# A graph layer on one core: layer 2 of the inner pairs with W2 standing and a split input, and half of the sums added by GpSimd

## What is computed

```python
h = jnp.maximum(_layernorm(x, axis=-1), 0.0)
agg = jax.ops.segment_sum(edge_attr, receivers, num_segments=N_NODES)   # receivers = dst
z = jnp.concatenate([agg, h], axis=1)
hid = jax.nn.relu(z @ W1 + b1)       # W1: 256 x 512
out = x + hid @ W2 + b2              # W2: 512 x 128
```

## Time and profile before

| | |
|---|---|
| median of 3 runs | 201.23 us |
| the profiled execution, its own time | 201.16 us |
| its span, first to last instruction | 199.3 us |
| PE busy, DVE busy, ACT busy, POOL busy | 96%, 66%, 43%, 22% |
| moved by DMA | 62.47 MB |
| granted TensorE clock, mean | 1.0 (2.4 GHz) |

### The profile page before, as it was taken

One profiled execution on the slowest core, in us unless ns is written; L12 is line 12 of the kernel. 1 busy time (PEld: TensorE's weight loads), 2 busy tenths in 40 slices (PEclk: granted clock), 3 DMA queues, 4 the chain that ended last, 5 costly groups with the idle time before them and its releaser, 6 DMA issues.

```text
span 199.3 us, 6821 instructions
## 1 busy us (share of the span) xinstructions
PE 190.6 (96%) x2568; PEld 163.2 (82%) x2568; DVE 131.8 (66%) x582; ACT 86.5 (43%) x188; POOL 43.4 (22%) x119
## 2 busy tenths in 40 slices
PE   7897899998999999999999999999999999999994
PEld 5586789776797898898898898898897898898894
DVE  2865775666877677678568669588487388575221
ACT  3454526433624634623714714813813704823440
POOL 6592202202211202210220220221121121220000
PEclk9999999999999999999999999999999999999999
DMA  6999999999999999999999999999999995010011
GB/s 203 382 374 378 362 373 377 375 375 377 376 377 376 375 379 383 383 392 387 381 378 388 377 385 380 376 385 378 341 376 378 311 376 167 4 53 3 0 53 44
DMA packets 44628, 62.47 MB, mean 313 GB/s; under 512 B 1822, under 2 KB 44300, under 8 KB 44594
## 3 DMA queue, kind: packets, MB, share of 16 engines
q1 hardware_dynamic: 44264, 61.66, 87.2%
q10 hardware_dynamic: 330, 0.36, 0.5%
HBM read 58.81 MB, written 3.20 MB: 311 GB/s over the span
## 4 chain that ended last, share of the span: by engine, by line
PE 79%; DMA 15%; SPq 2%; DVE 1%; issue 1%; DVEq 0%
PE bank L867 21%; PE bank L938 20%; PE bank L907 17%; PE bank L917 15%; DMA edges<-in_edge_attr 15%; PE bank L882 3%; PE bank L891 2%; SPq L303 1%; SPq L297 1%; DVE aggT L623 1%; DVE w_lo L642 0%; PE bank L860 0%; SPq L306 0%; PE bank L837 0%; SPq L327 0%
## 5 line engine op out<-in xcount | busy, mean ns | idle before, releaser
L867 PE MATMUL bank<-edges,onehot 128*32 128x128 f32 x1656 | 52.2, 275 | 2.7 <-DMA edges<-in_edge_attr 1.6
L867 PEld LDWEIGHTS bank<-edges,onehot 128*32 128x32 f32 x1656 | 43.1, 110 | 10.2 <-issue 6.2
L623 DVE TENSOR_TENSOR aggT<-bank,aggT 128x32 f32 x277 | 35.7, 190 | 22.2 <-issue 10.2
L458 ACT ACTIVATE hidden<-bank,b_col 128x512 f32<-128x512 f32 (+2 forms) x56 | 34.2, 634 | 35.9 <-PE bank L917 35.8
L938 PE MATMUL bank<-w,hidden 128*128 128x128 f32 (+1 forms) x392 | 47.6, 278 | 0.0
L938 PEld LDWEIGHTS bank<-w,hidden 128*128 128x128 f32 (+1 forms) x392 | 45.1, 191 | 2.2 <-issue 2.0
L426 ACT ACTIVATE xn<-xs,shift,rstd 128x128 f32<-128x128 f32 (+1 forms) x49 | 21.5, 485 | 49.7 <-POOL shift L383 49.6
L375 POOL TENSOR_SCALAR var<-meanvar 128x2 f32<-128x2 f32 (+1 forms) x25 | 7.9, 317 | 127.4 <-DVE meanvar L559 127.4
L539 DVE TENSOR_TENSOR onehot<-relT,iota 128x384 f32<-128x384 f32 x69 | 34.6, 550 | 0.0
L917 PE MATMUL bank<-agg_hi,w_hi 128*128 128x512 f32 (+2 forms) x56 | 21.5, 385 | 1.4 <-DVE agg_lo L583 1.4
L907 PE MATMUL bank<-hT_hi,w_hi 128*128 128x512 f32 (+2 forms) x56 | 22.2, 396 | 0.3 <-DVE hT_lo L576 0.3
(11 more groups left out here) (104 smaller groups left out, 178.6 us busy)
## 6 DMA issues: line engine op xcount, KB each, us to landing
edges<-in_edge_attr SPq DMA_DIRECT2D x69, 768.0 KB, 10.9
xs<-in_x SPq DMA_DIRECT2D x21, 128.0 KB, 9.8
out_rows<-xs SPq DMA_DIRECT2D x10, 256.0 KB
w<-in_L_gnn_W SPq DMA_DIRECT2D x3, 256.0 KB, 10.5
out_rows<-xs SPq DMA_DIRECT2D x4, 128.0 KB
xs<-in_x SPq DMA_DIRECT2D x1, 256.0 KB, 5.8
hidden<-in_dst SPq DMA_DIRECT2D x1, 192.0 KB, 2.8
hidden<-in_dst ACTq DMA_DIRECT2D x1, 192.0 KB, 4.5
```

Source lines behind the costliest of these rows:

```text
L458: nc.scalar.activation(hidden[:, t, 0:cols], hidden_of(s, t), ACT.Relu, bias=b1_col[:, t:t + 1]).then_inc(hidden_ready, 1)
L623: nc.vector.tensor_tensor(win, turn_ps[:, at:at + W], win, ALU.add).then_inc(agg_added, 1)
L867: ins = nc.tensor.matmul(sums_ps[t * W:(t + 1) * W, cols], onehot[:, hots, e, :], edges[:, slot, e * F:(e + 1) * F], start=(g == 0), stop= ...
```

## The change

- Layer 2 of the inner pairs (groups 3 to 12, `ONES <= n < NS - 1`) runs with W2 standing. W2 is split once into `w2_hi` and `w2_lo`. ScalarE writes the relu twice (`relu_split`), in full into what was W1's buffer, of two halves, and rounded into `hid_hi`; VectorE subtracts them into `hid_lo` (`rest_of_hidden`). TensorE multiplies 4 tiles times 3 products of 512 columns (`layer2_split`). The result stands with features as rows; ScalarE copies it and adds b2 (`out_copy`), TensorE transposes it one step later (`turn_out`, four of 128x128), and VectorE adds it to x (`finish`). `add_b2` is left out for those pairs.
- In odd steps from k = 7 on the turned sums of block k, the pair's second step apart, are copied from PSUM by ScalarE (`turned`), and GpSimd adds the chunks into `aggT` (`add_sums` in its list). The other half stays with VectorE.
- The rings `RING` and `HOTS` go from 8 to 6 slots to make room, W2's load moves ahead of round 6, and the stores of pairs come one step later. The lists of VectorE, ScalarE and GpSimd are reordered around it.

The diff, cut to its core:

```diff
-RING = 8
-HOTS = 8
+RING = 6
+HOTS = 6
...
-        ended = blocks_of(g)[-1] + 3
+        ended = blocks_of(g)[-1] + (3 if g < ONES else 4)
...
+            def add_sums(k):
+
+                first, last = chunks_by(k - 1), chunks_by(k)
+                _, bases = nc.values_load_multi_w_load_instructions(
+                    base_tab[0:1, first:last], engines=[pool.engine], min_val=0, max_val=N - 1,
+                    skip_runtime_bounds_check_because="clamped when written")
+                pool.wait_ge(turned_copied, (k - EARLY) // 2)
+                pool.wait_ge(agg_added, first)
+                order = list(range(first, last, 2)) + list(range(first + 1, last, 2))
+                for n, c in enumerate(order):
+                    if c == first + 1:
+                        pool.wait_ge(agg_added, first + n)
+                    win = aggT[:, bass.ds(bases[c - first], W)]
+                    at = (c - first) * W
+                    nc.gpsimd.tensor_tensor(win, turned[:, at:at + W], win, ALU.add).then_inc(agg_added, 1)
...
-            for b in range(2, NB):
+            for b in range(2, EARLY + 4):
                 spread(b)
+            for k in range(EARLY + 2, NB):
+                if group1(k) is not None:
+                    if k + 2 < NB:
+                        spread(k + 2)
+                    add_sums(k)
+                    if k + 3 < NB:
+                        spread(k + 3)
...
+            def relu_split(n, s):
+
+                if n == ONES:
+                    act.wait_ge(w1_ready, 2)
+                for t in range(HT):
+                    act.wait_ge(hidden_summed, n * HT + t + 1)
+                    if t == 0:
+                        act.wait_ge(out_summed, n)
+                    if n > ONES or t >= 2:
+                        act.wait_ge(hidden_lo_ready, (n - ONES) * HT + t - 1)
+                    nc.scalar.activation(full[:, t % 2, :], hid_ps[t][:, :], ACT.Relu, bias=bias_col[:, t:t + 1])
+                    nc.scalar.activation(hid_hi[:, t, :], hid_ps[t][:, :], ACT.Relu,
+                                         bias=bias_col[:, t:t + 1]).then_inc(hidden_ready, 1)
+
+            def out_copy(n):
+                act.wait_ge(out_summed, n + 1)
+                nc.scalar.activation(outT[:, :], out_ps[:, :], ACT.Identity,
+                                     bias=bias_col[:, HT:HT + 1]).then_inc(outT_ready, 1)
...
+                elif one is not None:
                     h_out(k)
-                if not early:
                     copy_sums(k)
-                round_agg(k - 1, chunks_by(k - 1), place(k - 1), group_of(k - 1))
-                if k == 1:
-                    h_out(2)
...
+                    round_agg(k - 1, chunks_by(k - 1), place(k - 1), group_of(k - 1))
+                    h_out(k + 1)
+                    n = len(ROUNDS[k]) * F
+                    act.wait_ge(sums_turned, k + 1)
+                    act.wait_ge(agg_added, chunks_by(k - 1))
+                    nc.scalar.activation(turned[:, 0:n], turn_ps[:, 0:n], ACT.Copy).then_inc(turned_copied, 1)
+                    relu_split(one, one)
+                else:
+                    copy_sums(k)
+                    if k + 1 < NB:
+                        normalise(k + 1)
+                    round_agg(k - 1, chunks_by(k - 1), place(k - 1), group_of(k - 1))
+                    out_copy(two)
+                    if k + 2 < NB:
+                        normalise(k + 2)
...
+                else:
+                    if k + 2 < NB:
+                        stats(k + 2)
+                    builds = ROUNDS[k + 1] if k + 1 < NB else []
+                    for t in range(HT):
+                        rest_of_hidden(two, t)
+                        if t < len(builds):
+                            build(builds[t])
+                        if t == 2:
+                            rest_of_h(k)
+                    rest_of_agg(k - 1, k - 1, place(k - 1))
...
+            def layer2_split(n):
+
+                pe.wait_ge(out_added, n)
+                for t in range(HT):
+                    pe.wait_ge(hidden_lo_ready, (n - ONES) * HT + t + 1)
+                    for i, (wt, v) in enumerate(((w2_hi, hid_hi), (w2_hi, hid_lo), (w2_lo, hid_hi))):
+                        ins = nc.tensor.matmul(out_ps[:, :], wt[:, t, :], v[:, t, :], start=(t == 0 and i == 0),
+                                               stop=(t == HT - 1 and i == 2))
+                ins.then_inc(out_summed, 1)
...
+                elif one is not None:
+                    sum_rounds(k)
+                    if one != ONES:
+                        turn_out(one - 1)
+                        layer1_h(one, one)
+                    turn_sums(k)
+                    turn_x(k + 1)
+                    layer1_agg(one, one, blocks_of(one)[-1] + 1)
                 else:
                     sum_rounds(k)
                     if k == FLAG + 1:
                         pe.wait_ge(over_read, 1)
-                    if two is not None:
-                        layer2(two, two)
-                    if one is not None and one != ONES:
-                        layer1_h(one, one)
+                    if two == ONES:
+                        pe.wait_ge(w2_ready, 1)
+                    layer2_split(two)
...
             layer1_h(NS - 1, NS - 1)
+            turn_out(NS - 2)
             layer1_agg(NS - 1, NS - 1, NB)
```

More of the change, by code:

```diff
@@ L589, in finish @@
                 bs = blocks_of(s)
-                if isinstance(n, int) and n < NS:
-                    dve.wait_ge(residual_ready, min(bs[-1] + 1, NB))
+                turned = isinstance(n, int) and ONES <= n < NS - 1
+                if isinstance(n, int) and n < NS and not turned:
+                    dve.wait_ge(residual_ready, n + 1 if n < ONES else ONES + 2)
                 if isinstance(s, int) and s == NS - 1:
```

167 lines of the change are left out of this document (108 added, 59 removed).

## The result

The changed kernel takes 206.0 us (median; 204.37 to 206.28 in four runs), the kernel before 201.15 (201.04 to 201.27, four runs beside it): ratio 1.0224, 95% interval 1.0171 to 1.0278. It is slower by 4.9 us, outside the range of the prediction. The profiled execution took 205.94 with a span of 204.2, against 201.16 and 199.3. Two details of the kernel, other than the account of the change has them: the kernel gives GpSimd its additions from step k = 5 on, not 7, and each of its ten sets has 12 of them, since the blocks with two rounds are even ones, whose 8 additions stay with VectorE.

A forecast was written before the change was run, and what follows sets the result against it. It took TensorE's list as the bound from 61.57 us almost to the end; -2.83 + 0.51 + 1.0 + 0.65 = -0.67 against 201.16 gave 200.5 us, likeliest 200.0 to 201.1, with a range of 199.0 to 204.3.

The forecast's parts named there:

- TensorE's list: TensorE's work per pair: layer 2 -0.77, turns +0.37, a pair from 14.82 to 14.42 us; -2.83 us in all.
- Who must keep up: Check that ScalarE, VectorE and GpSimd fit a 14.42 us pair; GpSimd's 12 additions were called the tight place.
- the ring: Way from one set of GpSimd's additions to the next, 9.1 us, plus 5.0 for the set: 14.1, or 14.75 with the check.
- the term of +0.65: Lateness of GpSimd's additions in five pairs with the window check: 5 x 0.33 = 1.65 us, less 1.0.
- that GpSimd is early: Claimed that GpSimd is 1.0 us early before the first pair with the window check, taken off its lateness.
- Rival 1: GpSimd's additions are late in every pair, from about 0.32 us an addition; 202.7 us as its middle, chance 0.25.
- pairs above 14.9: Stated sign that the forecast is wrong: a pair in the middle of the kernel takes more than 14.9 us.
- Step 19: VectorE must wait for and read three turned columns before making low parts: +1.0 us, bounds 0 and 2.0.
- The end: Group 12's layer 2 waits for slow relus, losing its gain (+0.07), and its result's turn adds 0.44: +0.51 us.
- Low parts "fit with 0.6 us": VectorE's last low part of a pair is done at 12.6 us, layer 2 wants it at 13.2: no loss.
- Rival 2: GpSimd's additions hold up VectorE, 0.15 us each, so low parts come late; 203 us, chance 0.12.
- Rival 3: Six ring slots starve TensorE of transfers: some 0.2 us a pair and 0.5 early; 202.5 us, chance 0.07.

The follow-up runs named there:

- a_ring: a_warm with two orders changed: in odd steps VectorE's statistics ahead of its builds, and GpSimd's load of places ahead of its wait; 202.65 us, ratio 1.0025.
- c_psum: a_ring with the low part taken straight from PSUM, ScalarE's 40 full relus dropped and four small matmuls correcting the output's bias; 200.64 us, ratio 0.9944.
- c_both: The changes of c_flag and c_psum together, on a_ring; 199.25 us median, ratio 0.9865 to the kernel before.
- a_warm: The changed kernel with 13 idle matmuls put into two TensorE gaps of step 1; 206.28 us, ratio 1.0208 to the kernel before.
- c_flag: a_ring with step 19's turned columns moved into the middle of layer 1's second half, in that step alone; 201.3 us, ratio 0.9981.
- a_vector: a_warm with GpSimd's additions and ScalarE's copy for them undone, VectorE adding all sums, layer 2 in its new form; 217.17 us, ratio 1.0745.
- b_six: The kernel before with rings of 6 slots instead of 8 and the loads of rounds 6 and 7 moved behind W2's and x's; 201.83 us, ratio 0.9995.

## Why the prediction was wrong

What was measured, step by step of the prediction.

- **TensorE's list: right.** Layer 2 takes 2.98 (3.00 predicted), the turn of its result 0.59 (0.60), and an undisturbed pair 14.41 (14.42), in a_ring, c_psum and c_both. But I took 14.42 for all pairs. Three of eight have a two-round block and a list of 13.67, so 0.74 us of the slack that I gave the ring wasn't there in them.
- **"Who must keep up": the ring was sized nearly right, and the term made of it was wrong.** The way to the set was to take 9.1 us, 9.75 with a piece of the check; it took 8.96 to 10.57. The set was to take 5.0; it took 4.67 to 5.50 (0.58 for an addition under VectorE's operations instead of 0.5, and less than 0.29 for one alone: 1.24 for six). But the term of +0.65 set this against 14.42 in every pair, priced every load of places at 0.92, where 1.66 and 2.02 came, and took 1.0 off "that GpSimd is early", where TensorE already waited 1.02 for GpSimd's first set. The six pairs from step 7 to step 19 took 89.06 us, the list is 4 x 14.41 + 2 x 13.67 = 84.98: **4.1 lost**. By pair it is 1.6 in the four ordinary ones, 1.6 in the two with a two-round block, whose list is shorter by 0.74 each while the ring isn't, and 0.85 by the slow load in step 9. a_warm, without that slow load, takes 88.21 for the same six pairs and a_ring 85.95: 2.3 are shown to be the ring's by order alone, 3.1 with the slow load, which stands in the ring too. This is the step that failed: +0.65 where the ring cost 3.3 from step 7 to step 23.
- **Rival 1, at 0.25, is what came, but not for its reason.** Its sign is there (ScalarE waits 9.6 us for GpSimd's additions, TensorE 2.0), and pairs above 14.9, the sign that the forecast is wrong, came too (15.31 and 15.16). But it needed an addition of 0.32 us or more that meets nothing, and such a one took 0.21. That it gave 203.8 at 0.40, the mean of what the trace shows (403 ns), is luck: that mean holds the waits beside VectorE, which the rival counts apart.
- **Step 19: +1.0 predicted.** With the ring out of the way (a_ring) the stretch takes 16.41 where the list has 14.41, and before it took 15.14 where its list had 14.83: 2.0 less 0.3, **+1.7**, near the upper bound of 2.0. c_flag gives 1.2 of it back by the place of the columns alone.
- **The end: right.** +0.51, and 0.37 for the turn of group 11's result, are 0.88; 23.4 against 22.5 is +0.9.
- **Low parts "fit with 0.6 us"**: in the ordinary pairs they do (a_ring). In the two-round pairs they don't, by 0.4 each (14.07 against 13.67): **+1.2**, a term that I did not have, again for want of the two-round pairs. c_psum takes it away. Of TensorE's waits for low parts (6.7 us in 12 waits) 3.9 us lie in step 19 and behind it.
- **The clock**: 0.7 us in the profile, by a_warm. Not predicted, and not the change's alone: a third of the runs of the kernel before had it beside my kernels, and three of the changed kernel's four. The one at full clock took 204.37, so the forecast of 200.5 fails without the clock too.
- **Rival 2**, VectorE held up by GpSimd: a build takes 564 ns on average and a low part 702; in a_vector, where GpSimd adds nothing, they take 550 and 684. That is 0.02 an operation on average (0.74 the longest low part of steps 11 and 12), where the rival needed 0.15. On the rule of the Trainium skill ("SBUF — State Buffer", "Who interferes with whom"), by which the loser is blocked for the whole instruction: the trace agrees for GpSimd, whose additions went through at about one for each of VectorE's operations (0.58 each, where builds and low parts start 0.53 to 0.66 apart), and c_psum agrees on the two SBUF inputs. It does not agree for VectorE, which was hardly held up.
- **Rival 3** fell with b_six.

The spans add up. From step 7's sums to step 23's it was 117.1 us before and is 119.7 after: eight pairs' list -3.3 (5 x 0.42 and 3 x 0.39), the ring with its slow load +3.3 (119.7 less a_ring's 116.4), step 19 +1.7, the two-round pairs +1.2, less 0.3 since the pair from step 7 now loses 0.14 over its list where it lost 0.43: +2.6. The end is +0.9. Up to step 7 it is +1.3: the clock is 0.7, the ring's first set 0.4 (a_ring starts step 7 at 59.98, a_warm at 60.39, and TensorE's wait for that set falls from 1.01 to 0.28), and 0.2 has not been taken apart. Together +4.8 of span; the medians differ by 4.9.

TensorE's list did get shorter by 0.4 us a pair, but until the ring is shortened too, as in a_ring, most of that doesn't show in the time: the list met a ring that was longer than it.

## What to carry to other kernels

When a bound engine's list gets shorter, write down every ring between the others (from the end of a set of operations to the end of the next, with the register loads and the spans of waiting between), and compare it with the shortest pair of that list, not the usual one: here a ring of 14.5 to 15.4 us stood against lists of 14.41 and 13.67, and decided more than the gain of 0.4 did. Look then at what stands in the ring without belonging to it: here statistics behind three builds and a load behind a wait cost 3 us together, and moving them was free. A helper engine's small operations are priced by whom they run beside: six cost 1.24 us alone and 3.49 beside VectorE's operations with two SBUF inputs, and taking one of those inputs from PSUM helped GpSimd more than cutting its width to a thirty-second.

## What I had not expected of the hardware

- GpSimd's addition of 128x32 takes 233 to 775 ns, median 254; of 128x1, 184 to 737, median 193. VectorE's operations beside it grow by some 3%. I had priced it by its width.
- The registers that VectorE loads for its additions' places cost 0.31 to 1.96 us (median 0.85, 15 loads), of one instruction form.
- The granted clock can fall to 1.2 GHz between 20 and 26 us (0.71 and 0.72 of two windows of 3 us), in one run and not in the next of the same kernel.
